# Second pass of a vision tower: side chains over more steps, next group's norm beside the forward scan

## Chip, cores and metric
The kernel runs on one core of one Trainium2 chip. The metric is the device time of one execution in microseconds, the median of several; less is better.

## What is computed
32 images of 96 x 96 are cut into 36 patches each, and with two leading tokens make sequences of 38 tokens of 192 features. Four layers follow, each added to its input after a layer norm: a gated state space layer, a mixture of 8 feed-forward experts (top 2), a bidirectional Mamba layer, and a mixture of 8 linear experts (top 2). The change touches the last two; the reference of the Mamba layer, cut:

```python
def _mamba(x, in_W, conv_w, conv_b, xproj_W, dt_W, dt_b, A_log, Dp, out_W):
    xz = x @ in_W
    xs, z = jnp.split(xz, 2, axis=-1)
...
    u = jnp.transpose(xc, (0, 2, 1))
    x_dbl = u @ xproj_W
    dt, Bm, Cm = jnp.split(x_dbl, [R, R + NS], axis=-1)
    dt = jax.nn.softplus(dt @ dt_W + dt_b)
    A = -jnp.exp(A_log)
    def step(h, inp):
        dt_t, B_t, C_t, u_t = inp
        dA = jnp.exp(dt_t[:, :, None] * A)
        h = dA * h + (dt_t * u_t)[:, :, None] * B_t[:, None, :]
        y = (h * C_t[:, None, :]).sum(-1)
        return (h, y)
...
    y = y * jax.nn.silu(z)
    return y @ out_W
h = x @ down_W + down_b
fwd = _ln(_mamba(h, f_in_W, f_conv_w, ...), f_ln_g, f_ln_b)
bwd = _ln(_mamba(h[:, ::-1], b_in_W, b_conv_w, ...), b_ln_g, b_ln_b)
y = fwd + bwd[:, ::-1]
return y @ up_W + up_b
...
h = h + _L0_attn_ref(_layernorm(h, axis=-1), ...)
h = h + _L0_ffn_ref(_layernorm(h, axis=-1), ...)
h = h + _L1_attn_ref(_layernorm(h, axis=-1), ...)
h = h + _L1_ffn_ref(_layernorm(h, axis=-1), ...)
```

The last mixture takes softmax and top 2 of 8 router scores, and sums the two chosen 192 x 192 products by their weights.

## The kernel before
The 32 images are 4 groups of 8, so a group has T = 304 tokens, features on partitions (128 "main" and 64 "rest"). A first pass does patches, the first scan and the routing of the expert layer; then 27 blocks of tokens go through the experts; the second pass, from about 584 us on, does the Mamba layer and the last mixture. Each engine has its own in-order program, and semaphores tie them.

A group's scan in one direction has 12 steps (QSTEPS). In step n SP reads two tiles of the rows (the step sizes into dA, the inputs into BB, L549; 4 slots, a slot is read again when the scan four steps before is done), ScalarE makes the decay (L813, two steps ahead), VectorE multiplies BB by B (b_product, L1145, one step ahead) and scans (L1159), GpSimd multiplies the states by C (product_step, L679) and TensorE adds them up over states (sum_step). The scan of step n needs the product of n - 2, that product the sum of n - 4 and its own scan.

Around the steps stand side chains, hung on them by hand, one behind another in each engine's program. part_a is the forward scan of group g, part_b the backward one. HOOKS maps step n to the place c of a chain: steps 0, 1, 2, 3, 5, 6, 7, 8. The chains are: the inputs of the next direction (TensorE: project_z, project_taps, project_states, project_steps; ScalarE: inputs, projected, raw_steps, softplus; VectorE: size_of_steps, steps), after which SP writes the rows of that direction to memory (write_rows) and waits for them; the output of the direction just finished (gated_output, direction_out, output_centre, direction_var, output_rstd, output_norm); for the group before, projection up, residual, norm, router, top-2 gates (gates_top, gates_weights, gates_rows), the gates' way through memory (write_gates, read_gates) and the mixture (gate_inputs L699 on GpSimd, mixture on TensorE, add_mixture on VectorE, L1398); for the next group, gathering of the expert rows, combine (L1388), turning back, residual (L1461), norm, projection down. In every engine a chain's place stands behind the scan, product or decay of its step; in TensorE mostly ahead of the sum. The mixture of group g - 1 runs in part_b of g, steps 4 to 9. Roots are computed as exp(-0.5 ln x): Ln and Exp each load a function table (ACT_TABLE_LOAD).

## Time and profile before
| | us |
|---|---|
| median of 3 runs | 1226.91 (1215.95 to 1231.17) |
| the profiled execution | 1218.23, its span 1216.5 |
| TensorE busy | 826.4 (68%) |
| VectorE busy | 711.5 (58%) |
| GpSimd busy | 471.1 (39%) |
| ScalarE busy | 447.5 (37%) |
| TensorE's mean granted clock | 0.767 of 2.4 GHz |

Engines in the rows: PE is TensorE's matmuls, PEld its weight loads, DVE VectorE, ACT ScalarE, POOL GpSimd, SP the engine that issues most transfers. One fp32 matmul appears as two records. An idle time in square brackets stands before the instruction and names what ended it. Times are from the start of the span.

### The profile page before, as it was taken

Reading aid. Unit: us, or ns where it says so; the run is one execution under the profiler, and the core shown is the slowest. Engines: PE = TensorE matmul, PEld = TensorE weight load, DVE = VectorE, ACT = ScalarE, POOL = GpSimd, SP = SyncE. Lnnn points to the kernel's source line nnn. Section 1 sums busy time; section 2 is a strip of 40 time slices with the busy share of each in tenths; the row PEclk is TensorE's granted clock in tenths of the full one; section 3 lists DMA queues with packets and bytes.
Section 4 is the critical chain, followed back from the end, with each engine's and each line's share of the span. In section 5 each row is a group of like instructions: output and inputs, shape, how many; then the busy total and the mean of one; then the engine's idle time right before and its main releaser. Section 6 shows DMA issues by size and latency. Waiting matters only on the chain.

```text
span 1216.5 us, 11333 instructions
## 1 busy us (share of the span) xinstructions
PE 826.4 (68%) x3666; PEld 584.5 (48%) x3666; DVE 711.5 (58%) x978; ACT 447.5 (37%) x847; POOL 471.1 (39%) x300
## 2 busy tenths in 40 slices
PE   3877768767544399999263686657876687657745
PEld 2543435434223388888142455444554465435423
DVE  3199898997982211111116956786748856587720
ACT  2345354444312122222135264545445451443130
POOL 0049446477562200000204634543626344235702
PEclk9778887777655699999676577867977787766957
DMA  9400100000000477676107735557345654347202
GB/s 366 199 30 0 38 1 11 14 1 24 1 4 21 147 227 227 227 227 191 31 16 189 191 103 149 131 145 186 84 124 141 181 127 119 90 131 208 54 0 70
DMA packets 55748, 134.59 MB, mean 111 GB/s; under 512 B 9439, under 2 KB 22150, under 8 KB 54934
## 3 DMA queue, kind: packets, MB, share of 16 engines
q1 hardware_dynamic: 51062, 127.45, 35.9%
q0 software_dynamic: 4496, 6.55, 2.1%
q8 instruction: 23, 0.38, 0.1%
q14 instruction: 23, 0.19, 0.1%
q10 hardware_dynamic: 144, 0.02, 0.0%
HBM read 115.82 MB, written 18.14 MB: 110 GB/s over the span
## 4 chain that ended last, share of the span: by engine, by line
PE 36%; DVE 28%; ACT 10%; issue 9%; DMA 8%; POOL 6%; SPq 2%; DVEq 0%; POOLq 0%; ACTq 0%
PE PS L1491 36%; DVE ST L1128 6%; DMA WXB<-ex_b 4%; DVE ST L1159 3%; DVE BB L1125 3%; POOL PR L679 2%; DVE BB L1121 2%; ACT L735 2%; DMA BB<-rows_d 2%; POOL slots_d L642 1%; DVE BB L1145 1%; POOL xp L665 1%; ACT dA L813 1%; DMA CR<-c 1%; DVE PR L1137 1%
## 5 line engine op out<-in xcount | busy, mean ns | idle before, releaser
L1491 PE MATMUL PS<-PR,CM 128*128 128x152 f32 (+1 forms) x512 | 156.8, 459 | 64.8 <-POOL PR L679 64.5
L1159 DVE TENSOR_TENSOR_SCAN ST<-dA,BB 128x608 f32<-128x608 f32 x96 | 172.2, 1800 | 25.1 <-issue 13.7
L1491 PEld LDWEIGHTS PS<-PR,CM 128*128 128x128 f32 x512 | 111.6, 254 | 100.9 <-POOL PR L679 76.8
L679 POOL TENSOR_TENSOR PR<-ST,q_V 128x608 f32<-128x608 f32 x48 | 86.7, 1814 | 186.1 <-DVE ST L1159 152.9
L813 ACT ACTIVATE dA<-dA,negA 128x304 f32<-128x304 f32 x192 | 93.1, 538 | 146.1 <-DMA BB<-rows_d 145.9
L1491 PE MATMUL PS<-p_S,SEL 128*64 128x152 bf16 (+1 forms) x576 | 83.7, 320 | 70.9 <-DVE PR L1137 37.7
L679 POOL TENSOR_TENSOR PR<-ST,p_V 128x608 f32<-128x608 f32 x48 | 85.3, 1780 | 118.5 <-DVE ST L1159 102.1
L620 POOL TENSOR_TENSOR aP<-dA,p_DL 128x912 f32<-128x912 f32 x32 | 74.4, 2325 | 136.0 <-DVE q_UP L1186 72.3
L912 ACT ACTIVATE HID<-PS,WX 128x128 f32<-128x128 f32 x162 | 47.6, 365 | 137.6 <-PE PS L1491 137.6
L1491 PEld LDWEIGHTS PS<-p_S,SEL 128*64 128x64 bf16 (+1 forms) x576 | 30.3, 120 | 130.6 <-issue 49.5
L1128 DVE TENSOR_TENSOR_SCAN ST<-aP,BB 128x912 f32<-128x912 f32 x32 | 89.2, 2789 | 1.1
L655 POOL DMA_DIRECT2D outs_d<-xp x27 | 14.6, 543 | 162.2 <-DVE xp L1343 162.2
L1491 PE MATMUL PS<-XT,WX 128*128 128x128 f32 x324 | 66.1, 286 | 14.8 <-DMA WXB<-ex_b 11.7
L1491 PE MATMUL PS<-WX,CM 128*128 128x304 f32 x192 | 60.2, 466 | 19.4 <-POOL WX L699 19.3
L1335 DVE COPY XT<-PS 128x128 f32<-128x128 f32 x27 | 7.9, 292 | 104.9 <-PE PS L1491 104.9
L1491 PE MATMUL PS<-HB,CM 96*128 96x152 f32 (+1 forms) x240 | 59.4, 418 | 7.6 <-DVE Or L1399 5.2
L1491 PE MATMUL PS<-XT,WXR 128*128 128x128 f32 x324 | 63.4, 278 | 0.0
L830 ACT ACTIVATE dA<-PS,neg_dt 128x608 f32<-128x608 f32 x64 | 37.4, 635 | 65.5 <-PE PS L1491 65.3
L1491 PEld LDWEIGHTS PS<-XT,WX 128*128 128x128 f32 x324 | 50.0, 195 | 22.1 <-issue 21.3
L1145 DVE TENSOR_TENSOR BB<-BB,q_R 128x608 f32<-128x608 f32 x48 | 45.6, 950 | 22.9 <-DMA BB<-rows_d 22.6
L1491 PEld LDWEIGHTS PS<-HB,CM 96*128 96x128 f32 x240 | 47.6, 240 | 21.3 <-issue 7.8
L1491 PEld LDWEIGHTS PS<-WX,CM 128*128 128x128 f32 x192 | 39.2, 210 | 37.7 <-POOL WX L699 24.4
(340 smaller groups left out, 1728.3 us busy)
## 6 DMA issues: line engine op xcount, KB each, us to landing
dA<-rows_d SPq DMA_DIRECT2D x96, 304.0 KB, 3.7
BB<-rows_d SPq DMA_DIRECT2D x96, 304.0 KB, 4.4
WX<-ex_m SPq DMA_DIRECT2D x27, 963.0 KB
slots_d<-WXR SPq DMA_DIRECT2D x8, 960.0 KB, 27.6
WXR<-ex_r SPq DMA_DIRECT2D x27, 192.0 KB
WX<-gates_d SPq DMA_DIRECT2D x4, 1216.0 KB, 7.4
CM<-c SPq DMA_DIRECT2D x1, 4430.0 KB, 19.8
xp<-x_p SPq DMA_DIRECT2D x4, 864.0 KB, 4.7
```

Of the source, the lines that this page charges most:

```text
L620: nc.gpsimd.tensor_tensor(aP[:, c % 2], dA[:, c % 2], P.DL[:, :].unsqueeze(1).broadcast_to([128, NC, PK]), ALU.mult).then_inc(ap_ready.sem, 1)
L679: nc.gpsimd.tensor_tensor(PRq[:, c % 2], STq[:, c % 2], DIRS[k].Cw.unsqueeze(1).broadcast_to([128, QB, T]), ALU.mult).then_inc(q_product.s ...
L735: nc.scalar.activation(s.RS[0:rows, :], s.VE[0:rows, :], ACT.Exp, scale=-0.5).then_inc(rstd.sem, 1)
L813: last = nc.scalar.activation(dAq[:, slot, i, :], dAq[:, slot, i, :], ACT.Exp, scale=negA[:, j:j + 1])
L830: last = nc.scalar.activation(dA[:, c % 2, :, cols], PS[:, A_BANK:A_BANK + NC, cols], ACT.Exp, scale=neg_dt0[:, h:h + 1])
L912: last = nc.scalar.activation(HX[:, p, f, :], PS[:, WIDE_BANK + 2 * p + h, j * 128:(j + 1) * 128], ACT.Gelu, bias=WX[:, p, FFN + FT * D + ...
L1121: nc.vector.tensor_tensor(BB[:, c % 2], P.WV[:, :].unsqueeze(1).broadcast_to([128, NC, PK]), PS[:, B_BANK:B_BANK + NC, 0:PK], ALU.mult).th ...
L1125: nc.vector.tensor_tensor(BB[:, c % 2], BB[:, c % 2], dA[:, c % 2], ALU.mult).then_inc(b_times_a.sem, 1)
L1128: nc.vector.tensor_tensor_scan(flat(ST, False), flat(aP[:, c % 2], False), flat(BB[:, c % 2], False), 0.0, ALU.mult, ALU.add).then_inc(P.s ...
L1145: nc.vector.tensor_tensor(BBq[:, slot], BBq[:, slot], DIRS[k].Bw.unsqueeze(1).broadcast_to([128, QB, T]), ALU.mult).then_inc(b_times_w.sem, 1)
L1159: nc.vector.tensor_tensor_scan(flat(STq[:, c % 2], back), flat(dAq[:, slot], back), flat(BBq[:, slot], back), 0.0, ALU.mult, ALU.add).then ...
L1491: return nc.tensor.matmul(out, lhsT, rhs, start=first, stop=last)
```

## The change
second_pass now runs part_a once more ahead and once more behind, and part_a gets two more groups: nxt, whose combine, residual and mean now stand in the forward scan at steps 8 to 11 (before: steps 0 to 2 of the backward scan), and mix, whose mixture is finished there. HOOKS is gone; each link of a chain has its own step, one link per step. The norms' roots of the group before and of the next are done together at step 1 of part_b (both_powers), and the logarithm of the step sizes together with the root of the output norm (step_logs), Ln beside Ln and Exp beside Exp. ScalarE writes the size of the steps (Abs) where VectorE did. Top-2 gates move from part_a to steps 4 to 6 of part_b. The six parts of the mixture move from steps 4 to 9 of part_b to its steps 10 and 11 and steps 0 to 3 of the following part_a. The sums of the two directions get a bank each, and the chains banks 5, 7, 4 and 1. TensorE takes the last sum of a direction between z and taps of the next. SP writes the rows of the next direction one step earlier, ahead of its last read, and reads the gates behind them.

```diff
-MIX_PARTS, MIX_FROM = 6, 4
-HOOKS = {0: 0, 1: 1, 2: 2, 3: 3, 5: 4, 6: 5, 7: 6, 8: 7}
+MIX_PARTS, MIX_FROM = 6, QSTEPS - 2
...
-        Y_BANK = 3
+        Y_BANK = (3, 0)
...
-        X_BANK, Z_BANK, AFTER_BANK = 6, (5, 7), (7, 5)
+        X_BANK, Z_BANK, AFTER_BANK, L_BANK, Q_BANK, QR_BANK = 6, 5, 1, 5, 7, 4
...
         def second_pass(eng, part_a, part_b):
 
-
-
-
+            def near(g):
+                return g if 0 <= g < GROUPS else None
+
+            part_a(None, None, 0, None)
             part_b(None, None, 0)
-            part_a(0, None)
-            part_b(0, None, 1)
-            for g in range(1, GROUPS - 1):
-                part_a(g, g - 1)
-                part_b(g, g - 1, g + 1)
-            part_a(GROUPS - 1, GROUPS - 2)
-            part_b(GROUPS - 1, GROUPS - 2, None)
-            part_a(None, GROUPS - 1)
+            for g in range(GROUPS):
+                part_a(g, near(g - 1), near(g + 1), near(g - 2))
+                part_b(g, near(g - 1), near(g + 1))
+            part_a(None, GROUPS - 1, None, GROUPS - 2)
             part_b(None, GROUPS - 1, None)
+            part_a(None, None, None, GROUPS - 1)
...
             load_next(0)
+            write_rows(0, 0)
             for g in range(GROUPS):
-                write_rows(g, 0)
+                rows_there(g, 0)
                 for c in range(QSTEPS):
+                    if c == QSTEPS - 1:
+                        write_rows(g, 1)
                     read_rows(g, 0, c)
-                    if c == 7 and g >= 2:
+                    if c == 10 and g >= 2:
                         store(g - 2)
-                if g >= 2:
-                    store_end(g - 2)
-                write_rows(g, 1)
+                rows_there(g, 1)
                 for c in range(QSTEPS):
+                    if c == QSTEPS - 1 and g:
+                        write_gates(g - 1)
                     read_rows(g, 1, c)
-                    if g and c == SLOTS:
-                        write_gates(g - 1)
-                    if g and c == SLOTS + 1:
-                        read_gates(g - 1)
-                if g + 2 < GROUPS:
-                    load_next(g + 1)
+                    if c == 4:
+                        if g >= 2:
+                            store_end(g - 2)
+                        if g + 2 < GROUPS:
...
+            def part_a(g, tail, nxt, mix):
+                for n in range(QSTEPS):
+                    if g is not None:
+                        product_step(g, 0, n)
+                    if nxt and n == 4:
+                        pool.wait_ge(rows_ready.sem, rows_ready.after(nxt, 1))
+                        pool.sem_inc(turn_taken, 1)
+                    if nxt and n in (4, 5, 6):
+                        gather(nxt, (n - 4,))
+                    if mix is not None and n + QSTEPS - MIX_FROM < MIX_PARTS:
+                        gate_inputs(mix, n + QSTEPS - MIX_FROM)
+
             def part_b(g, tail, nxt):
-                for c in range(QSTEPS):
+                for n in range(QSTEPS):
                     if g is not None:
-                        product_step(g, 1, c)
-                    if tail is not None and 0 <= c - MIX_FROM < MIX_PARTS:
-                        gate_inputs(tail, c - MIX_FROM)
+                        product_step(g, 1, n)
+                    if tail is not None and n >= MIX_FROM:
+                        gate_inputs(tail, n - MIX_FROM)
 
...
+            def both_powers(t, x):
+
+                for s, g, bank in ((Q, t, Q_BANK), (L, x, L_BANK)):
+                    if g is not None:
+                        act.wait_ge(s.ln_var.sem, s.ln_var.after(g, 1))
+                        log_of(s, 128, bank, s.ln_log)
+                for s, g in ((L, x), (Q, t)):
+                    if g is not None:
+                        power_of(s, 128, s.ln_log, s.ln_rstd, g, 1)
 
...
+                    last = nc.scalar.activation(DIRS[k].TM[:, cols], PS[:, Z_BANK, cols], ACT.Abs, bias=cm(d + "dtb", h, h + 1))
...
-            def softplus(g, k):
-
-                s = DIRS[k]
-                act.wait_ge(abs_dt.sem, abs_dt.after(g, k + 1))
-                nc.scalar.activation(s.OM[:, :], s.TM[:, :], ACT.Exp, scale=-1.0).then_inc(exp_dt.sem, 1)
-                act.wait_ge(exp_dt.sem, exp_dt.after(g, k + 1))
-                nc.scalar.activation(LZ, s.OM[:, :], ACT.Ln, bias=1.0).then_inc(log_dt_ready.sem, 1)
+            def step_logs(g, k, out):
+
+                if g is not None:
+                    s = DIRS[k]
+                    act.wait_ge(dt_raw.sem, dt_raw.after(g, k + 1))
+                    nc.scalar.activation(s.OM[:, :], s.TM[:, :], ACT.Exp, scale=-1.0).then_inc(exp_dt.sem, 1)
+                if out is not None:
+                    act.wait_ge(bn_var.sem, bn_var.after(*out))
+                    log_of(Q, BN, AFTER_BANK, bn_log)
+                if g is not None:
+                    act.wait_ge(exp_dt.sem, exp_dt.after(g, k + 1))
+                    if k or not is_first(g):
+                        act.wait_ge(Q.w_ready.sem, Q.w_ready.after(g, k))
+                    nc.scalar.activation(LZ, s.OM[:, :], ACT.Ln, bias=1.0).then_inc(log_dt_ready.sem, 1)
+                if out is not None:
+                    power_of(Q, BN, bn_log, bn_rstd, *out)
...
-            def part_a(g, tail):
+            def part_a(g, tail, nxt, mix):
                 for n in range(QSTEPS):
-                    c = HOOKS.get(n)
                     if g is not None:
                         direction_step(g, 0, n)
-                    if tail is not None and n == 0:
-                        if tail:
-                            add_mixture(tail - 1)
-                        gated_output(tail, 1)
+                    if mix is not None and n == 5:
+                        add_mixture(mix)
+                    if g is not None and n == 6:
+                        if tail is not None:
+                            dve.wait_ge(out_mm.sem, out_mm.after(tail, 2))
+                        steps(g, 1)
                     if tail is not None:
-                        if c == 1:
+                        if n == 1:
+                            gated_output(tail, 1)
+                        if n == 3:
                             output_centre(tail, 1)
-                        if c == 2:
+                        if n == 6:
...
-                        if c == 4:
-                            centre(Q, Q, tail, 0, 5)
-                        if c == 7:
-                            links[Q] = 0
-                            gates_top(Q, tail, 4)
-                    if g is not None:
-                        if c == 3:
-                            size_of_steps(g, 1)
-                        if c == 5:
-                            if tail is not None:
-                                dve.wait_ge(out_mm.sem, out_mm.after(tail, 2))
-                            steps(g, 1)
-                        if c == 2 and not is_last(g):
-                            find_rows(g + 1)
-                    if tail is not None:
-                        if c == 3:
+                        if n == 7:
...
+                        if n == 9:
+                            centre(Q, Q, tail, 0, Q_BANK)
                     if nxt is not None:
-                        if c == 0:
+                        if n == 2 and nxt:
+                            find_rows(nxt)
+                        if n == 8:
                             combine(nxt)
-                        if c == 1:
+                        if n == 10:
                             dve.wait_ge(M.back_T.sem, M.back_T.after(nxt, 1))
                             dve.wait_ge(h_loaded.sem, h_loaded.after(nxt, 32))
                             if g is not None:
...
-                        if c == 2:
-                            centre(L, L, nxt, 0, 5)
-                        if c == 3:
-                            scale(L, nxt, 0)
-                        if c == 5:
-                            size_of_steps(nxt, 0)
-                        if c == 7:
+                        if n == 11:
+                            centre(L, L, nxt, 0, L_BANK)
+
+            def part_b(g, tail, nxt):
+                for n in range(QSTEPS):
+                    if g is not None:
+                        direction_step(g, 1, n)
+                        if n == 1:
+                            gated_output(g, 0)
+                        if n == 3:
+                            if tail is not None:
+                                dve.wait_ge(Q.ln_x.sem, Q.ln_x.after(tail, 1))
+                            output_centre(g, 0)
+                    if nxt is not None and n == 2:
+                        scale(L, nxt, 0)
+                    if tail is not None:
+                        if n == 2:
+                            scale(Q, tail, 0)
+                        if n == 4:
+                            links[Q] = 0
+                            gates_top(Q, tail, QR_BANK)
+                        if n == 5:
+                            gates_weights(Q, tail)
+                            assert links[Q] == Q.chain.per_group, ("Q", links[Q])
+                        if n == 6:
+                            gates_rows(Q, tail, Q_BANK)
+                    if n == 7:
+                        if nxt is not None:
                             if g is not None:
                                 dve.wait_ge(out_mm.sem, out_mm.after(g, 1))
                             steps(nxt, 0)
-                    if g is not None:
-                        if c == 1:
...
+            def part_a(g, tail, nxt, mix):
+                    if n == 0:
+                        if g is not None:
+                            pe.wait_ge(dt_raw.sem, dt_raw.after(g, 1))
+                            project_z(1).then_inc(in_mm.sem, 1)
+                        if tail is not None:
+                            sum_step(tail, 1, QSTEPS - 1)
+                        if g is not None:
+                            pe.wait_ge(bc_copied.sem, bc_copied.after(g, 2))
+                            project_taps(1).then_inc(in_mm.sem, 1)
+                        if n == 2:
+                        if n == 3:
+                            direction_mean(tail, 1)
+                        if n == 5:
+                            direction_var(tail, 1)
+                        if n == 7:
+                            pe.wait_ge(final.sem, final.after(tail, 0))
+                            pe.wait_ge(y_sum.sem, y_sum.after(tail, 1))
+                            mm(PS[:, Q_BANK, 0:T], cm("up", 0, DM, p=BN), YS[:, 0, :], True, True)
+                            mm(PS[:, QR_BANK, 0:T], cm("up", DM, DM + 128, p=BN), YS[:, 0, :], True, True).then_inc(up_proj.sem, 1)
+                        if n == 8:
+                            pe.wait_ge(Q.residual.sem, Q.residual.after(tail, 1))
+                            mean(Q, Q, tail, 0, Q_BANK)
+                        if n == 11:
+                            variance(Q, tail, 0, Q_BANK)
+                    if g is not None:
+                        if n == 3:
+                            project_states(g, 1)
+                        if n == 4:
+                            project_steps(g, 1)
+                    if nxt is not None:
+                        if n == 9:
+                            if g is not None:
+                                pe.wait_ge(dt_raw.sem, dt_raw.after(g, 2))
+                            pe.wait_ge(mixed.sem, mixed.after(nxt, TILES))
+                            back(M, nxt, L_BANK, QR_BANK)
+                        if n == 11:
+                            pe.wait_ge(M.residual.sem, M.residual.after(nxt, 1))
+                            mean(L, L, nxt, 0, L_BANK)
+                    if mix is not None and n + QSTEPS - MIX_FROM - 1 < MIX_PARTS:
+                        mixture(mix, n + QSTEPS - MIX_FROM - 1)
```

SP at the boundary from group 1 to group 2, before. L549 is a read of rows for a step, L534 to L536 are writes of rows, L505 to L509 the load of the next group; the gates of group 0 were read 7 pairs of rows earlier.

```order
L549 DMA BB<-rows_d 128x1x608
L505 DMA KEEP<-keep_d 102x60
L508 DMA m_Hm<-h_md 128x304
L509 DMA m_Hr<-h_rd 64x304
L534 DMA rows_d<-q_DL 128x304
L535 DMA rows_d<-q_DL 64x152
L536 DMA rows_d<-q_DL 64x152
L534 DMA rows_d<-q_WV 128x304
L535 DMA rows_d<-q_WV 64x152
L536 DMA rows_d<-q_WV 64x152
L549 DMA dA<-rows_d 128x1x608
```

The same place now (L548 is the read of rows, L531 to L533 the writes, L553 writes the gates, L558 and L562 read them).

```order
L553 DMA gates_d<-q_LW 8x304
L548 DMA dA<-rows_d 128x1x608
L548 DMA BB<-rows_d 128x1x608
L531 DMA rows_d<-q_DL 128x304
L532 DMA rows_d<-q_DL 64x152
L533 DMA rows_d<-q_DL 64x152
L531 DMA rows_d<-q_WV 128x304
L532 DMA rows_d<-q_WV 64x152
L533 DMA rows_d<-q_WV 64x152
L558 DMA WX<-gates_d 128x2432
L562 DMA WX<-gates_d 64x4x304 x2
L548 DMA dA<-rows_d 128x1x608
```

The gates of group 0 have moved from the middle of the backward reads to the front of the next group's first rows.

TensorE at the head of group 2's forward scan, before. PR are sums of the scan, HB z and taps, p_WV and HID the output product, p_UP and p_Xm the projections, WX the mixture.

```order
L1491 MATMUL PS<-WX,CM 128x304 x4
L1491 MATMUL PS<-PR,CM 128x152 x4
L1491 MATMUL PS<-HB,CM 128x304
L1491 MATMUL PS<-HB,CM 128x152 x2
L1491 MATMUL PS<-HB,CM 128x304 x4
L1491 MATMUL PS<-HB,CM 128x152 x8
L1491 MATMUL PS<-PR,CM 128x152 x4
L1491 MATMUL PS<-p_WV,CM 96x304
L1491 MATMUL PS<-HID,CM 96x304
L1491 MATMUL PS<-p_V,ones_bn 96x304
L1491 MATMUL PS<-p_UP,CM 128x304
```

And now.

```order
L1501 MATMUL PS<-HB,CM 128x304
L1501 MATMUL PS<-HB,CM 128x152 x2
L1501 MATMUL PS<-PR,CM 128x152 x4
L1501 MATMUL PS<-HB,CM 128x304 x4
L1501 MATMUL PS<-HB,CM 128x152 x8
L1501 MATMUL PS<-WX,CM 128x304 x4
L1501 MATMUL PS<-PR,CM 128x304 x2
L1501 MATMUL PS<-WX,CM 128x304 x4
L1501 MATMUL PS<-p_WV,CM 96x304
L1501 MATMUL PS<-HID,CM 96x304
L1501 MATMUL PS<-PR,CM 128x304 x2
L1501 MATMUL PS<-WX,CM 128x304 x4
```

The last sum of the backward scan stands between z and taps, the output product has a sum and two mixture parts ahead of it, and a mixture part stands behind each of the first sums.

TensorE in the backward scan of group 1, now: what stands ahead of the logits turned round (CM,q_LW), for which VectorE's gates_top waits.

```order
L1501 MATMUL PS<-q_Xm,CM 128x304
L1501 MATMUL PS<-q_Xr,CR 128x304
L1501 MATMUL PS<-PR,CM 128x304 x2
L1501 MATMUL PS<-HB,CM 128x304
L1501 MATMUL PS<-HB,CM 128x152 x2
L1501 MATMUL PS<-HB,CM 128x304 x4
L1501 MATMUL PS<-HB,CM 128x152 x8
L1501 MATMUL PS<-CM,q_LW 102x8 x3
```

Before, it stood in the forward scan, with a sum between.

```order
L1491 MATMUL PS<-q_Xm,CM 128x304
L1491 MATMUL PS<-q_Xr,CR 128x304
L1491 MATMUL PS<-PR,CM 128x304 x2
L1491 MATMUL PS<-CM,q_LW 102x8 x3
L1491 MATMUL PS<-PR,CM 128x304 x2
```

Z and taps have come between the router's product and the turned logits.

## Rows read from the trace of the kernel before

**Rows 1.** Stretches: us, busy time of each engine, granted clock, DMA share, GB/s.

```profile
646.20:690.30 44.10, 24.15 (x66) 15.87 (x66) 37.92 (x36) 19.76 (x37) 27.31 (x17) 0.65 0.68 172
690.30:750.60 60.30, 42.38 (x138) 29.11 (x138) 40.73 (x51) 31.13 (x55) 22.64 (x13) 0.70 0.48 123
750.60:815.90 65.30, 41.21 (x142) 29.33 (x142) 46.51 (x75) 32.10 (x58) 30.84 (x19) 0.79 0.57 147
815.90:881.60 65.70, 50.72 (x188) 36.18 (x189) 47.57 (x52) 30.14 (x53) 31.99 (x19) 0.84 0.55 143
881.60:952.30 70.70, 47.41 (x149) 33.14 (x147) 48.14 (x77) 32.09 (x58) 30.84 (x19) 0.74 0.52 133
952.30:1018.00 65.70, 50.82 (x188) 36.31 (x189) 48.38 (x52) 30.13 (x53) 33.20 (x19) 0.84 0.52 139
1018.00:1093.40 75.40, 49.36 (x149) 34.60 (x147) 44.97 (x71) 32.10 (x58) 21.21 (x13) 0.70 0.45 119
1093.40:1146.10 52.70, 37.59 (x124) 26.32 (x125) 45.13 (x33) 15.63 (x30) 38.10 (x19) 0.77 0.59 154
1146.10:1216.50 70.40, 37.64 (x106) 22.32 (x104) 12.30 (x42) 10.05 (x16) 11.22 (x8) 0.64 0.12 34
```

**Rows 2.** VectorE's waits, 646.2 to 1146.1 us: total, times, longest.

```profile
DVE p_TM L1228 <- PE PS L1491: 21.1, 3, 10.0
DVE q_Cm L1245 <- ACT q_RS L735: 20.4, 7, 5.8
DVE BB L1145 <- DMA BB<-rows_d: 16.5, 12, 3.2
DVE q_TM L1205 <- ACT q_DL L797: 14.3, 3, 5.5
DVE ST L1159 <- issue: 13.7, 2, 7.0
```

**Rows 3.** Timeline of TensorE and ScalarE, group 1: start, duration, instruction.

```profile
754.07 6.19 PE L1491 MATMUL PS<-HB,CM 96*128 96x304 f32 x30
...
839.95 0.75 PE L1491 MATMUL PS<-m_Xm,CM 128*96 128x304 f32 x2 [2.24 <-DVE m_Xr L1025]
...
861.13 2.21 PE L1491 MATMUL PS<-WX,CM 128*128 128x304 f32 x8
...
863.75 0.58 ACT L806 ACTIVATE aP<-q_OM 128x456 f32<-128x456 f32 x1
```

**Rows 4.** Timeline of VectorE, scans of groups 0 and 3.

```profile
679.71 2.69 DVE L1159 TENSOR_TENSOR_SCAN ST<-dA,BB 128x608 f32<-128x608 f32 x1
683.00 2.68 DVE L1159 TENSOR_TENSOR_SCAN ST<-dA,BB 128x608 f32<-128x608 f32 x1
...
1127.26 2.69 DVE L1159 TENSOR_TENSOR_SCAN ST<-dA,BB 128x608 f32<-128x608 f32 x1
...
1131.78 2.68 DVE L1159 TENSOR_TENSOR_SCAN ST<-dA,BB 128x608 f32<-128x608 f32 x1
```

**Rows 5.** Timeline, group 1 backward: a free product and a free scan.

```profile
831.82 1.47 POOL L679 TENSOR_TENSOR PR<-ST,p_V 128x608 f32<-128x608 f32 x1 [2.77 <-DVE ST L1159]
...
830.32 1.42 DVE L1159 TENSOR_TENSOR_SCAN ST<-dA,BB 128x608 f32<-128x608 f32 x1
```

**Rows 6.** Side work, group 1: gates (as Rows 1), then groups: busy us, mean ns, idle.

```profile
803.70:809.20 5.50, 2.65 (x13) 1.75 (x12) 4.57 (x23) 1.20 (x4) 1.44 (x2) 1.00 0.51 170
...
L735 ACT ACT_TABLE_LOAD x4 | 5.1, 1283 | 0.1
...
L1214 DVE TENSOR_TENSOR p_OM<-p_OM,p_TM 128x456 f32<-128x456 f32 x1 | 0.6, 634 | 0.0
```

**Rows 7.** Transfers: issues with median us to landing; timeline at the group boundary.

```profile
WX<-gates_d SPq DMA_DIRECT2D x2, 304.0 KB, 10.0
...
873.76 0.32 SPq L534 DMA_DIRECT2D rows_d<-q_DL  x1
...
883.26 1.66 DVE L1145 TENSOR_TENSOR BB<-BB,q_R 128x608 f32<-128x608 f32 x1 [1.68 <-DMA BB<-rows_d]
```

289 lines of the change are left out of this document (114 added, 175 removed).

## Prediction
> **What bounds the kernel now.** I read first the table of stretches, cut at the end of every twelfth scan of the second pass [rows 1]. The eight half-passes take 44.1, 60.3, 65.3, 65.7, 70.7, 65.7, 75.4 and 52.7 us, 499.9 us together; what is ahead of them (646.2 us) is not touched by the change, and 70.4 us follow. VectorE is the busiest engine of every half, but in the six middle ones it stands still for 17 to 30 us (span less busy time). TensorE's granted clock is 0.65 to 0.84 of full, so it spends part of each half at 1.2 GHz and the rest at 2.4 GHz.
>
> Then the waits of VectorE over the eight halves [rows 2]. They aren't for data of the scan, apart from 16.5 us for rows from memory. They are for side work: the gated output waits for TensorE (21.1 us in 3), the root of the output norm for ScalarE (20.4 us in 7), the raw step sizes for ScalarE (14.3 us in 3), and a scan that waits behind the same queue (13.7 us in 2, named "issue"). The longest of each are 10.0, 5.8, 5.5 and 7.0 us. In the backward scan of group 1 it is the pair of 7.0 and 5.5 us: TensorE works through down, z, taps, projections and mixture, 24.4 us from the first of them to the end of the logarithm that they feed (839.95 to 864.33) [rows 3]. At the head of a forward scan it is the sums that stand behind z and taps.
>
> Then what a scan step costs if no side work is late. Two steps without any are 3.29 us apart (679.71 to 683.00) [rows 4]: product 0.7, scan 1.4, and 1.27 us in which the scan is held (2.69 instead of 1.42). In that time GpSimd's own product runs, which takes 1.47 us alone [rows 5]. With a gate input as well on GpSimd the steps are 4.52 us apart (1127.26 to 1131.78) [rows 4], 1.24 more. Where a side operation lies between, GpSimd's product can be over before the scan, and the scan takes 1.42 [rows 5].
>
> That two-input VectorE operations and GpSimd's exclude each other is also what the Trainium skill says (SBUF — State Buffer, Who interferes with whom), and that a VectorE operation with one SBUF input does not; the trace agrees with the first by the 2.69 us, and with the second by the operations that read PSUM at their usual time. The rule speaks against the change: the closer the steps, the more scans are held.
>
> **The change part by part.**
> The bare cost of a half is 12 x 3.28 = 39.4 us. To it comes VectorE's side work [rows 6]: the gates 4.6 busy and some 0.8 between them, 5.4 us, steps 3.4 (four operations of the size of p_OM's 0.63 and some short ones), the gated output 2.0 (three such), combine 1.8, and a scale, centring, norm or residual 0.8 to 1.0 each, two or three operations of under 0.5. Of it some 5 us a half read PSUM and can lie beside GpSimd's product; I take 3 us off for that, between nothing (if they fall at other times) and 5.
>
> The size of the steps leaves VectorE (one operation of 0.63 us, twice a group) and becomes two short ones on ScalarE, hidden in its idle time (it is busy 30 to 32 us of 65 [rows 1]). The roots of the two layer norms share one pair of table loads, the step logarithm and the output's root another. A table load costs 1.28 us, and in group 1 four stand before the Exp of L735 alone [rows 6]; by the order of the instructions 16 loads a group become 10. So 7.7 us of ScalarE's time go, on the path only where VectorE waits for a root, which the new places avoid anyway: none in the sum.
>
> The Trainium skill (ScalarE: Activation LUTs, Table sets) says that one set holds exp and ln, so that ln and then exp would need one load. The trace does not show that: each Exp behind an Ln has its own load. By the page the pairing would save less; the sum takes nothing from it either way.
>
> Now the work that stays, half by half, before and after. "Small" is 1.5 us a half for waits under a microsecond, as those of the residual now (0.7 to 1.3 us).
> - Group 0 forward, 44.1: gets combine, residual and centring of group 1. 39.4 + find 0.9 + steps 3.4 + 3.5 - 3 + small 1.5 + first rows 1.8 = 47.5.
> - Group 0 backward, 60.3: 39.4 + 2.0 + scale 0.8 + 0.4 + 3.4 + 0.8 - 3 + small 1.5, and a wait of 4 us at step 7: down to logarithm took 24.4 us with 3.2 of mixture in it [rows 3], so 21 or 22, and steps 3 to 7 give 18. 49.5.
> - Group 1 forward, 65.3: side work 13.2. No mixture. 39.4 + 13.2 - 3 + 1.5, plus 4 for the gathers on GpSimd, which put 3 us each on steps 4 to 6. 55.5.
> - Groups 1 and 2 backward, 65.7 each: side work 14.0, two gate inputs 2.5, small 1.5. New wait at step 4: VectorE's top-2 choice wants the logits turned round, which TensorE now does behind z and taps (30 records in 6.19 us at best [rows 3]). I take 5 us, between 3.5 (full clock) and 11 (half). And 1 us for the gates at step 10. 60.5.
> - Group 2 forward, 70.7: side work 14.1, four gate inputs 5.0, small 1.5. SP puts the read of the gates (1216 and twice 304 KB, up to 10.0 us to landing [rows 7]) ahead of the first rows of the next group. Counted from step 7: the steps take 4 us, then 9.5 us from their last write to the first product over new rows (873.76 to 883.26 [rows 7]), and 8 more for the gates: 21.5. The four last scans with two gate inputs end at 4 + 13.1 + 2.5 = 19.6. Wait 2. TensorE has z, taps, five mixture parts, projections and five sums in the first five steps: 6.2 + 5 x 2.1 + 4 + 1.4 + 5 x 1.05, 27 us at full clock (a mixture part is 8 records in 2.21 us, a sum half of that [rows 3]), against 22 to 26 on VectorE: a wait of 5, between 0 and 15, and 0.5 in the sum for rounding. 64.5.
> - Group 3 forward, 75.4: the same with side work 9.7: 60.
> - Group 3 backward, 52.7: side work 9.4, two gate inputs instead of six, small 1.5, gates 1. 39.4 + 9.4 - 3 + 2.5 + 2.5 = 51, and 0.5 for the mixture's first part: 51.5.
>
> Sum 47.5 + 49.5 + 55.5 + 60.5 + 64.5 + 60.5 + 60 + 51.5 = 449.5, so 50 us off. The tail grows: mixture parts of group 2 (2.2 us each at full clock, some 4 at 1.2 GHz) now stand in TensorE's queue before the last group's output product, mean and variance, and four gate inputs run behind the last product: 8 us, between 4 and 16. The final mixture and its gates' way through memory stay. 1218.2 - 50 + 8 = **1176 us**. The profiled execution of 1218.2 lies 0.7% under the median of 1226.9, and above the lowest, 1216.0.
>
> **The rivals.**
> - *Stalls only move.* Five stages per group are handed over in order on four in-order queues, and one late link (the logits behind the taps, the sums behind the mixture) holds all. For: the 5 and 15 us ends above. If they come at their upper ends (11 instead of 5 in two backward halves, 15 instead of 5 in two forward ones, tail 14) it is 1176 + 12 + 20 + 6 = 1214: no difference. Against: the waits of up to 10.0 us for the gated output vanish whatever comes, since the gated output is asked for a step later and the sums come ahead of the taps.
> - *The gates' read starves the rings.* If rows only start when the gates have landed (10.0 us), both group boundaries cost 8 us more: 1192. Still faster.
> - *The packing is better than thought.* If the side work covers GpSimd's product in most steps (5 us a half in place of 3) and the small waits are none: 1176 - 28 = 1148.
> - *Slower: TensorE falls to 1.2 GHz in the busiest halves.* Its work in a forward half with mixture is about 39 us at full clock and 78 at half, above the 64 planned; a backward one has 62. Then each of groups 2 and 3 forward takes 78 (+31), the three waits at step 4 and the tail double (+18), and the chain at step 7 is late in groups 0 to 2 (+20): 1245. It decides from where the granted clock of these halves is under 0.6; now they have 0.70 to 0.84, and closer packing gives TensorE less idle time, which speaks against it.
>
> **How the numbers follow.** The forecast (1155 to 1200) gets 0.55, better packing 0.12, the starved rings 0.08, moved stalls 0.17, slower 0.08. The range that leaves out 2 in 10 is 1145 to 1212. A measurement of this kernel, whose three runs span 1.2%, can tell about 2% from no change. Against 1226.9, faster is under 1202: 0.55 + 0.12, and most of the ring case, 0.72; same 0.20; slower 0.08.
>
> **What would show it.** In the profile after: VectorE's waits for L1228, for the output's root and for raw steps shrink to under 3 us each; a new wait at the first gate operation behind a PSUM copy (logits turned), of some 5 us in groups 1 and 2; the last two halves about 60 and 51 us; more scans at 2.69 us than now; 16 loads fewer on ScalarE; the tail at 78 us. Wrong would be: a clock under 0.65 in a middle half, VectorE idle for over 8 us before the add of the mixture at step 5, first rows more than 5 us behind the last scan, or a forward half of group 1 above 60 us.

## The result, and the profile after

The changed kernel takes 1144.23 us (median of 4 runs, 1140.57 to 1146.81), against 1225.1 us (median of 4 by now, 1215.95 to 1231.17) before: a ratio of 0.934 (95% interval 0.928 to 0.941). That is faster, as forecast, but by 81 us where 51 were forecast (1226.9 to 1176), and 0.8 us under the range's lower end (1145). The sum itself started from the profiled execution of 1218.2 us: it took 42 us off, and the profiled execution after (1143.86 us) is 74 us shorter.

The table of stretches of the kernel after, cut again at the end of every twelfth scan (columns as in [rows 1]):

```profile
651.35:696.50 45.15, 26.72 (x73) 17.75 (x74) 41.76 (x43) 23.16 (x45) 26.97 (x17) 0.61 0.76 189
696.50:744.10 47.60, 32.08 (x131) 23.72 (x130) 40.29 (x43) 27.73 (x51) 25.62 (x12) 0.82 0.63 160
744.10:796.20 52.10, 36.21 (x152) 26.72 (x151) 48.77 (x59) 26.30 (x52) 32.69 (x19) 0.85 0.67 171
796.20:847.90 51.70, 34.11 (x135) 24.45 (x134) 45.21 (x67) 28.81 (x55) 24.73 (x12) 0.81 0.62 162
847.90:909.40 61.50, 47.30 (x203) 34.60 (x203) 51.25 (x61) 27.19 (x54) 41.97 (x25) 0.91 0.67 169
909.40:961.00 51.60, 35.62 (x136) 25.56 (x134) 45.29 (x68) 28.81 (x55) 24.75 (x12) 0.80 0.59 158
961.00:1017.50 56.50, 44.66 (x186) 32.50 (x185) 47.38 (x46) 26.19 (x52) 32.28 (x19) 0.94 0.67 169
1017.50:1064.10 46.60, 27.52 (x85) 18.58 (x85) 44.37 (x58) 19.75 (x36) 27.54 (x13) 0.71 0.68 174
1064.10:1142.00 77.90, 46.86 (x153) 31.07 (x153) 15.41 (x42) 10.05 (x16) 20.16 (x14) 0.74 0.11 30
```

The eight halves are 412.7 us together, 87.2 less than the 499.9 of [rows 1]. VectorE's busy time in them (third number after the length) is 364.3 us, before 359.4: its work has not fallen. What it stood still has, from 140.5 us to 48.4. The tail is 7.5 us longer. The first scan starts 5.2 us later, at 651.35 in place of 646.2; 4.7 us of that lie in code that the change doesn't touch. VectorE's last copy of the expert blocks, 0.36 us long, starts at 580.55 before and here at

```profile
585.22 0.36 DVE L1360 COPY xp<-PS 128x192 f32<-128x192 f32 x1 [2.70 <-PE PS L1501]
```

4.7 us later. In the 18 profiled executions below and above (one for each kernel), this copy starts anywhere from 580 to 589 us and the first scan starts from 646 to 656 us, so the start is left out where kernels are compared: "halves" is the time from the first scan to the end of the last. The first half, which begins with the first rows, still varies from 44.8 to 47.0 us between kernels that are alike in it; the last one is 46.6 in eleven of them. A difference in the halves of under 2 us is therefore read without the first half.

VectorE's waits in the halves of the kernel after (total, times, longest), to be read against [rows 2]:

```profile
DVE BB L1166 <- DMA BB<-rows_d: 15.4, 8, 5.6
DVE ST L1180 <- POOL PR L684: 9.4, 7, 1.5
DVE q_gate L1074 <- PE PS L1501: 7.9, 2, 4.1
DVE Om L1415 <- PE PS L1501: 2.4, 2, 1.3
...
DVE p_TM L1229 <- ACT p_OM L819: 1.4, 1, 1.4
DVE q_OM L1231 <- ACT aP L827: 1.4, 1, 1.4
```

Gone are the gated output's wait for TensorE (21.1 us), that for the output's root (20.4), for the raw steps (14.3) and the scans that stood behind the same queue (13.7). Rows from memory are as late as before (15.4 for 16.5), in fewer and longer waits. New is the forecast wait for the turned logits.

### The profile page after: what moved, and what is told of

Read it like the earlier page. It is cut to its first block, busy times and chain, and to the rows that moved or that the text cites. A ratio compares the mean times of both kernels' runs of the same rounds, so it can differ in the third digit from the quotient of the medians.

```text
span 1142.0 us, 11341 instructions
## 1 busy us (share of the span) xinstructions
PE 773.1 (68%) x3666; PEld 556.8 (49%) x3666; DVE 715.8 (63%) x970; ACT 433.3 (38%) x847; POOL 479.6 (42%) x300
## 4 chain that ended last, share of the span: by engine, by line
DVE 31%; PE 30%; issue 12%; DMA 10%; POOL 9%; ACT 6%; SPq 2%; DVEq 0%; POOLq 0%; ACTq 0%
PE PS L1501 29%; DVE ST L1149 6%; DMA WXB<-ex_b 5%; DVE ST L1180 5%; POOL PR L684 4%; DVE BB L1146 3%; DMA BB<-rows_d 3%; DVE BB L1142 2%; DVE BB L1166 2%; POOL slots_d L647 2%; DMA CR<-c 1%; DMA xp<-outs_d,slot_u 1%; POOL q_TM L618 1%; DVE PR L1158 1%; POOL xp L670 1%
## 5 line engine op out<-in xcount | busy, mean ns | idle before, releaser
L1501 PE MATMUL PS<-PR,CM 128*128 128x152 f32 (+1 forms) x512 | 149.6, 440 | 99.2 <-POOL PR L684 99.0
L1180 DVE TENSOR_TENSOR_SCAN ST<-dA,BB 128x608 f32<-128x608 f32 x96 | 166.5, 1739 | 10.9 <-POOL PR L684 9.4
L1501 PEld LDWEIGHTS PS<-PR,CM 128*128 128x128 f32 x512 | 103.0, 237 | 135.4 <-POOL PR L684 115.4
L684 POOL TENSOR_TENSOR PR<-ST,p_V 128x608 f32<-128x608 f32 x48 | 106.5, 2228 | 94.6 <-DVE ST L1180 91.9
L684 POOL TENSOR_TENSOR PR<-ST,q_V 128x608 f32<-128x608 f32 x48 | 84.3, 1759 | 130.4 <-DVE ST L1180 125.7
L1501 PEld LDWEIGHTS PS<-p_S,SEL 128*64 128x64 bf16 (+1 forms) x576 | 29.9, 119 | 134.8 <-issue 48.4
L1166 DVE TENSOR_TENSOR BB<-BB,q_R 128x608 f32<-128x608 f32 x48 | 51.6, 1076 | 25.8 <-DMA BB<-rows_d 25.5
L1501 PE MATMUL PS<-WX,CM 128*128 128x304 f32 x192 | 54.5, 434 | 9.4 <-POOL WX L692 9.4
L1501 PE MATMUL PS<-WX,HID 128*128 128x192 f32 x324 | 57.1, 326 | 0.0
L1501 PEld LDWEIGHTS PS<-WX,HID 128*128 128x128 f32 x324 | 53.5, 190 | 0.0
L1501 PEld LDWEIGHTS PS<-XT,WXR 128*128 128x128 f32 x324 | 51.9, 202 | 0.0
```

The lines of the kernel that those rows point to most:

```text
L684: nc.gpsimd.tensor_tensor(PRq[:, c % 2], STq[:, c % 2], DIRS[k].Cw.unsqueeze(1).broadcast_to([128, QB, T]), ALU.mult).then_inc(q_product.s ...
L1166: nc.vector.tensor_tensor(BBq[:, slot], BBq[:, slot], DIRS[k].Bw.unsqueeze(1).broadcast_to([128, QB, T]), ALU.mult).then_inc(b_times_w.sem, 1)
L1180: nc.vector.tensor_tensor_scan(flat(STq[:, c % 2], back), flat(dAq[:, slot], back), flat(BBq[:, slot], back), 0.0, ALU.mult, ALU.add).then ...
L1501: return nc.tensor.matmul(out, lhsT, rhs, start=first, stop=last)
```

## The experiments

All medians are of four or ten runs; the kernel before, run beside them, had medians of 1218 to 1223 us. "Halves" and waits come from one profiled execution of each kernel, and "more" or "less" is against the kernel after (412.7 us), for labels that begin with b_ against the kernel before (499.9 us). First what the holding by GpSimd costs, since the prediction charged it to every scan.

**short_product**

```diff
-                nc.gpsimd.tensor_tensor(PRq[:, c % 2], STq[:, c % 2], DIRS[k].Cw.unsqueeze(1).broadcast_to([128, QB, T]),
+                nc.gpsimd.tensor_tensor(PRq[:, c % 2, :, 0:16], STq[:, c % 2, :, 0:16], DIRS[k].Cw[:, 0:16].unsqueeze(1).broadcast_to([128, QB, 16]),
```

> The changed kernel (1144.2 us), with GpSimd's product of states and C over 16 of the 304 columns of each block; the rest of the product is left out, so GpSimd no longer holds VectorE in the second pass (but for the gate inputs). It prices all holding at once. The prediction's sum had 12 x 3.28 - 3 = 36.4 us a half for products and scans where VectorE alone needs 12 x 2.1 = 25.2: 11.2 us x 8 = 90 us. If that is what holding costs, the time falls by about 90 us, to 1054. The theory now is that side operations cover GpSimd's product, so that less is held: VectorE's busy time in the eight halves is 364 us now, products and scans free of holding (202) and the side work by the prediction's list (90) make 292, so at most 72 us can go, and as some comes back as waits for rows (2.74 us a step when they are read back to back) I expect -50 to -65, 1079 to 1094.

1100.05 us (1098.35 to 1102.38), halves 370.3. The stretches of group 1 backward and group 2 forward (51.7 and 61.5 us in the kernel after):

```profile
785.40:829.40 44.00, 31.57 (x137) 23.45 (x136) 36.83 (x67) 29.47 (x57) 11.50 (x12) 0.86 0.70 183
829.40:885.90 56.50, 46.08 (x202) 34.69 (x202) 41.87 (x60) 26.45 (x53) 20.01 (x25) 0.96 0.74 192
```

VectorE's busy time falls by 80.5 us over the eight halves (364.3 to 283.8), more than the 72 that I took for the most, yet the halves fall by 42.4 only: waits grow from 48.4 to 86.6 us. Of the 80.5 us that GpSimd takes from VectorE, 38 come back as waits. Waits for rows are the largest of the new ones:

```profile
DVE BB L1166 <- DMA BB<-rows_d: 29.8, 20, 8.1
```

So neither the prediction's price (90 us of time) nor my second guess (50 to 65) was right; it is 44, and that is the most that holding can cost here, since the cut product also hands its result to TensorE earlier.

How much of VectorE's work is held, and where, follows from its busy time for the scans and for the products BB by B alone (this tile's instructions, over the halves; length, then busy time). Before, after, and short_product:

```profile
646.10:1146.10 500.00, 260.12 (x191) 0.76 0.54 139
651.30:1064.10 412.80, 248.80 (x191) 0.81 0.66 169
652.90:1023.30 370.40, 205.34 (x191) 0.85 0.73 187
```

So of the 80.5 us, 43.5 lie on scans and products (248.8 less 205.3), and 37.0 on all the side work (115.5 less 78.5, the rest of 364.3 and 283.8).

**close_output**: the output's chain is put together again, several hand-overs a step.

```diff
-                        if n == 3:
+                        if n == 2:
                             output_centre(tail, 1)
-                        if n == 6:
+                        if n == 3:
                             output_norm(tail, 1)
...
-                        if n == 5:
-                            direction_var(tail, 1)
+                        if n == 3:
+                            direction_var(tail, 1)
```

(the same in part_b, the mean on TensorE and the squares on ScalarE at step 2, and the root on ScalarE at step 3 by itself, with its own Ln and Exp)

> The changed kernel with the spreading of one chain undone: the output of a direction has its product and mean on TensorE at step 2, squares on ScalarE and centring on VectorE at step 2, variance, root and norm at step 3, several hand-overs within a step as before; its root has its own Ln and Exp. Before, VectorE waited 20.4 us in 7 for this root and 7.0 in 4 for the centring. If spreading is what removed these waits, they come back at 2 to 4 us in each of seven halves: the halves' sum (412.7) goes to 427 to 440, the time to 1158 to 1170. The rival: VectorE has other work queued and the waits only change places with others: within 5 us of 1144.

1169.11 us (1166.93 to 1172.19), halves 440.1, 27.4 more. VectorE's waits grow by 35 us while its busy time falls by 8 (364.3 to 356.6); one line holds most of them:

```profile
DVE q_Cm L1264 <- ACT q_RS L742: 30.1, 7, 6.7
```

and the timelines of VectorE and ScalarE in group 1's backward scan show why a step is too short for it:

```profile
818.96 1.42 DVE L1182 TENSOR_TENSOR_SCAN ST<-dA,BB 128x608 f32<-128x608 f32 x1
823.33 0.47 DVE L1264 TENSOR_TENSOR q_Cm<-q_Cm,q_RS 96x304 f32<-96x304 f32 x1 [2.96 <-ACT q_RS L742]
...
818.37 0.46 ACT L863 ACTIVATE q_RS<-q_Cm 96x304 f32<-96x304 f32 x1 [3.35 <-DVE q_Cm L1258]
818.74 0.97 ACT L836 ACTIVATE dA<-dA,negA 128x304 f32<-128x304 f32 x2
819.73 1.28 ACT L738 ACT_TABLE_LOAD   x1
821.02 0.51 ACT L738 ACTIVATE q_VE<-PS,eps_col 96x304 f32<-96x304 f32 x1
821.55 1.28 ACT L742 ACT_TABLE_LOAD   x1
822.84 0.46 ACT L742 ACTIVATE q_RS<-q_VE 96x304 f32<-96x304 f32 x1
```

Squares, decay, load, Ln, load and Exp take 4.9 us on ScalarE (818.37 to 823.30); VectorE has a product and a scan to do meanwhile, 2.1 us. Given three steps or four, as in the change, none of it is seen.

**norm_backward**: combine, residual and mean of the next group back in the backward scan, and its chain two steps later.

```diff
-                        if n == 8:
+                        if n == 8 and g is None:
                             combine(nxt)
...
+                    if nxt is not None and late:
+                        if n == 0:
+                            combine(nxt)
...
-                    if n == 7:
+                    if n == 7 + late:
```

(The two norms' roots are taken apart at three boundaries, and SP's store_end and load_next move from step 4 to 7 with it.)

> The changed kernel with one part undone: combine, residual and mean of the next group at steps 0, 1 and 2 of the backward scan, as before, and what hangs on them two steps later (scale at 4, inputs at 6, size of the steps and the output's norm at 9); each link still has a step of its own. VectorE's work is the same. If it is the early start of this chain that lets the spread chains end in time, the rows of the next group are written two steps (8 to 10 us) later, and the wait for the first rows grows by that at three boundaries: 24 to 30 us, 1168 to 1175, the heads of groups 1 to 3. The rival: where the norm stands doesn't matter once every link has its own step: 1150 or less.

1171.6 us (1168.86 to 1173.27), halves 436.4, 23.7 more. Its waits for rows:

```profile
DVE BB L1172 <- DMA BB<-rows_d: 34.6, 11, 11.3
```

19.2 more than after. The start of the chain in the forward scan, and so the time at which SP can write the next rows, is worth what was expected (24 to 30 us; 27 by the medians).

**b_hooks_spread**: the kernel before, with its chains over more steps and nothing else.

```diff
-HOOKS = {0: 0, 1: 1, 2: 2, 3: 3, 5: 4, 6: 5, 7: 6, 8: 7}
+HOOKS = {0: 0, 1: 1, 3: 2, 4: 3, 6: 4, 8: 5, 9: 6, 10: 7}
```

> The kernel before (1225 us) with one idea of the change alone: the eight places of the chains over more steps (0, 1, 3, 4, 6, 8, 9, 10 instead of 0, 1, 2, 3, 5, 6, 7, 8), nothing else moved. The halves have 17 to 30 us in which VectorE stands still for side work. If the gain of the change is mostly that each link has a step or more between it and the next, this gives a large part of it: 25 to 45 us, 1180 to 1200. The rival: the later chains end later too (rows of the next direction written after the scan's end), so the wait moves to the first rows of each half: 1215 to 1240.

1231.16 us (1228.84 to 1240.72), a ratio of 1.014 (1.005 to 1.023) to the kernel before; halves 506.2, 6.3 more. Two lines of its waits:

```profile
DVE BB L1145 <- DMA BB<-rows_d: 47.9, 14, 8.5
...
DVE q_Cm L1245 <- ACT q_RS L735: 9.6, 4, 3.9
```

The root's wait is halved (20.4 in [rows 2]), but that for rows trebles (16.5): the rival. Spreading these eight places alone doesn't pay; with the earlier start that norm_backward takes away, it does.

**b_sum_first**, **sum_behind_taps** and **sum_late_gated_early** are about the last sum of the backward scan. b_sum_first is the kernel before with this alone:

```diff
                 if g is not None:
                     project_z(1).then_inc(in_mm.sem, 1)
+                if tail is not None:
+                    sum_step(tail, 1, QSTEPS - 1)
+                if g is not None:
                     pe.wait_ge(bc_copied.sem, bc_copied.after(g, 2))
                     project_taps(1).then_inc(in_mm.sem, 1)
-                if tail is not None:
-                    sum_step(tail, 1, QSTEPS - 1)
```

> The kernel before (1225 us) with one part of the change alone: TensorE takes the last sum of the backward scan between z and taps of the next. VectorE's wait for it was 21.1 us in 3. With the sum ahead of the taps (24 of 30 records) the wait loses the taps' 4 to 7 us each at TensorE's clock there: 12 to 21 us, 1204 to 1213, if nothing else is late then. The rival: it is the chain behind the taps (inputs, projections, raw steps, root of the output) that holds the head, and the wait only moves to those: 1220 or more.

1204.2 us (1195.03 to 1211.23), 0.989 (0.985 to 0.993) of before; halves 478.4, 21.5 less, and the wait is 7.4 us in 2. The profiled execution is the fastest of its ten (1195.03 us); by the medians the gain is 15 us.

```profile
DVE p_TM L1228 <- PE PS L1491: 7.4, 2, 4.2
```

sum_behind_taps is the changed kernel with the reverse of this diff.

> The changed kernel with one part undone: TensorE takes the last sum of the backward scan behind z and taps, as before, not between them. Before, VectorE waited 21.1 us in 3 for that sum (10.0 at the longest). The gated output now stands at step 1, one step later. Taps are 24 records, 4.3 us at full clock. If the order is what removed the wait, it comes back at some 3 us in each of groups 1 to 3, 9 to 12 us, 1153 to 1156; the fallback is the later gated output: if that alone covers it, 1144 to 1147.

1145.62 us (1143.68 to 1148.5), halves 412.1: nothing lost, and the later gated output is enough alone. sum_late_gated_early adds

```diff
-                        if n == 1:
+                        if n == 0:
                             gated_output(tail, 1)
```

> The changed kernel with two parts undone: the last sum of the backward scan behind z and taps, and the gated output that reads it at VectorE's step 0, not 1. With the sum behind the taps alone nothing was lost (halves 412.1 in place of 412.7), while in the kernel before the sum ahead of them alone won 21.5 us of its halves. If either of the two is enough to hide the sum, this one shows the wait again: 4 to 6 us in each of groups 1 to 3, halves 425 to 431, 1156 to 1162. The rival: the wait was of TensorE's other load in the kernel before, and is gone whatever the order: within 3 us of 1144.

1150.04 us (1147.5 to 1154.74), halves 419.6, 6.9 more (1.6 of them in the first half, which the edit doesn't reach), and `p_TM` waits again:

```profile
DVE p_TM L1245 <- PE PS L1501: 8.5, 3, 3.6
```

Two parts of the change act on the same wait, and with the later gated output in place the sum's order gives nothing; the reverse, the sum first with the gated output early, was not run in the changed kernel. With both gone it is 5 to 7 us, half of what I expected or less. That TensorE has less ahead of it than in the kernel before would explain this, but it wasn't tested.

**short_mixture** and **b_short_mixture** leave most of the mixture out, of the kernel after and of before:

```diff
                 for i in (2 * part, 2 * part + 1):
+                    if part and part < MIX_PARTS - 1:
+                        continue
...
-                nc.gpsimd.tensor_tensor(GX[:, 2 * part:2 * part + 2, :], GX[:, 2 * part:2 * part + 2, :],
+                nc.gpsimd.tensor_tensor(GX[:, 2 * part:2 * part + 2, 0:16], GX[:, 2 * part:2 * part + 2, 0:16],
```

> The changed kernel with most of the last mixture left out: gate inputs over 16 of 304 columns, and TensorE's products of parts 1 to 4 of 6. The forward halves of groups 2 and 3 (61.5 and 56.5 us) have mixture, that of group 1 (52.1) has none. The prediction took 5 us of gate inputs and 5 of waiting for TensorE for it. If the sum over VectorE's and GpSimd's work is right, group 2 falls to 52 to 53, group 3 to 48 to 49 (4 us less side work), and the tail loses 8 us of gate inputs and 9 of products: together 30 to 38 us, 1106 to 1114. The rival: what lengthens these halves is the gates' read, which stays in: group 2 stays above 57.

1125.46 us (1120.35 to 1130.13), halves 405.6: group 2's forward half 57.7, group 3's 52.6, each 3.8 less where I expected 9 and 8. VectorE's busy time there falls by 5.7 and 8.3 us (51.25 to 45.52, 47.38 to 39.07), so the gate inputs take what the prediction charged (5 us) or more; waits take part of it back. In the three backward halves for which the prediction charged 2.5 us each VectorE's busy time doesn't move (45.21 and 45.26, 45.29 and 45.24, 44.37 and 44.47). That group 2 stays at 57.7 is the rival's number, with 6.3 us of waits for rows at its head as before (6.0), and the rest of it stays open. Of the 18 us that the profiled execution lacks, 11 lie in the tail (66.9 in place of 77.9).

> The kernel before with most of the last mixture left out, as in the run of the changed kernel: gate inputs over 16 of 304 columns, and TensorE's products of parts 1 to 4 of 6. There its halves fell by 6.6 us (412.7 to 406.1). Here the mixture stands beside down, z, taps and projections of the backward scan, 24.4 us from down to the logarithm with 3.2 of mixture in it. If its move to the forward scan is a part of the gain, its price is larger here: the three backward halves of groups 1 to 3 lose 5 to 8 us each, 15 to 24 together. The rival: it is hidden there as well, and the halves fall by less than 7.

1203.09 us (1197.29 to 1210.01), halves 486.0, 13.9 less; the backward halves of groups 1 to 3 lose 6.6, 3.7 and 7.3, 17.6 together, and group 2's forward half gains 4.9. By the halves the mixture cost 14 us where it stood and costs 7 where it stands. The medians don't bear this out: the whole time falls by 15.5 us here and by 18.8 in the changed kernel, and 10.1 and 11.0 of that lie in the tails, which leaves 5 and 8 for the rest. What its move is worth, between nothing and 7 us, is not shown.

**gates_later** reads the gates behind the second pair of the next rows, **gates_early** ahead of the writes:

```diff
-                if g + 1 < GROUPS:
-                    write_rows(g + 1, 0)
                 if g:
                     read_gates(g - 1)
+                if g + 1 < GROUPS:
+                    write_rows(g + 1, 0)
```

> The changed kernel with the gates read behind the second pair of rows of the next forward scan instead of ahead of the first, and the six mixture parts at steps 0 to 5 of that scan (GpSimd) and 1 to 6 (TensorE), the addition at step 7. If the read of the gates (1.8 MB) is what keeps the first rows back (VectorE waits 4.3, 1.3 and 0.4 us for them at the head of group 2), the waits for rows, 15.4 us in 8, fall by 8 to 10 us, and the time to 1134 to 1137. The rival: the read takes the same share of the queues a few steps later, and the waits for rows move to steps 3 to 5, or the addition waits at step 7: 1141 to 1150.

1149.63 us (1147.28 to 1152.71), halves 419.1, 6.4 more: the wait for rows is one of 4.6 us at the head of group 2, in place of 4.3, 1.3 and 0.4, and GpSimd's and TensorE's mixture is later by a step and a half.

> The changed kernel with one move on SP: the gates are read ahead of the writes of the next rows, not behind them. SP waits 3 to 5 us for those rows (from 832.7 to 837.0 in group 1's backward scan), and the read of the gates would lie in that time. If the read beside the first rows is what holds the heads of groups 2 and 3 (VectorE waits there 4.3 + 1.3 + 0.4 us for rows), each loses 3 to 5 us and the halves' sum falls from 412.7 to 403 to 407. The rival, from the last kernel with the gates read later (heads no shorter: one wait of 4.6 in place of 4.3 + 1.3 + 0.4): the way from the last write through memory to the first product over new rows (10 us) is the bound there, and the halves stay within 2 us.

1141.68 us (1139.75 to 1144.64), halves 411.7; group 2's forward half is 61.4, group 3's 54.7. SP's own timeline around it:

```profile
835.60 0.60 SPq L548 DMA_DIRECT2D BB<-rows_d  x1
837.87 0.34 SPq L558 DMA_DIRECT2D WX<-gates_d  x1
838.25 1.30 SPq L562 DMA_DIRECT2D WX<-gates_d  x2
840.53 0.33 SPq L531 DMA_DIRECT2D rows_d<-q_DL  x1
...
843.43 0.62 SPq L533 DMA_DIRECT2D rows_d<-q_WV  x1
848.57 0.56 SPq L548 DMA_DIRECT2D dA<-rows_d  x1
```

The rows are now written beside the gates' read: SP's first read of rows follows 4.5 us after the end of its last write, where it follows 2.1 us after it in the changed kernel, with the issues of the gates between. VectorE waits 2.3 and 1.4 us at that head and not 6.0 in all, but group 2's half is as long; only group 3's is 1.8 shorter. The wait is paid in other places.

**logits_first** moves logits_T on TensorE ahead of z and taps; **both_moves** is this with gates_later, **early_and_logits** with gates_early.

> The changed kernel with one move on TensorE: the logits turned round stand ahead of z and taps at step 4 of the backward scan, not behind. VectorE waits for them 7.9 us in 2 (4.1 the longest). If the order on TensorE is the cause and nothing else is as late, both waits go and the time falls by 6 to 8 us, to 1136 to 1138. The rival: z, taps and the chain behind them (inputs, projections, raw steps, logarithm) are as late, so the wait turns up at step 7 before the size of the steps, and in more held scans: 1141 or more.

1145.02 us (1141.86 to 1148.95), halves 413.3, of which the first half is 1.6 more than after. The wait for the logits is gone, and the two backward halves lose 1.3 and 1.0 us, not 4. Two lines of its waits:

```profile
DVE ST L1180 <- POOL PR L684: 12.3, 9, 1.5
...
DVE q_gs L1096 <- ACT q_gs L778: 3.8, 2, 2.0
```

The next link (the ratio on ScalarE) is late instead, by 1.9 us each.

> The two moves together: logits turned ahead of z and taps, and gates read behind the second pair of rows with the mixture one and a half steps later. If both waits are independent and on the path, the gains add: 14 to 18 us, 1126 to 1130. If each only uncovers the other's slack, no more than the larger of the two, about 1136.

1148.47 us (1143.41 to 1149.04), halves 420.0: no sum of gains.

> The changed kernel with two moves: gates read ahead of the writes of the next rows, and the logits turned round ahead of z and taps. Alone the first gave 1.7 us in the halves and the second none (2.3 us less in two backward halves, 1.6 more elsewhere). If gains add it is 1139 to 1142; the rival, that each frees time that the next link takes, 1142 to 1145.

1140.38 us (1137.48 to 1142.41), halves 412.4. Without the first half, its halves are 1.6 us less than those of the changed kernel (gates_early alone: 2.3 less, logits_first: 1.0 less); the medians differ by 0.3%, which the start's scatter covers.

**unpaired** takes the two norms' roots one behind the other, each with its Ln and Exp, **one_bank** lets both directions sum into one bank:

```diff
-                for s, g, bank in ((Q, t, Q_BANK), (L, x, L_BANK)):
+                for s, g, bank in ((L, x, L_BANK), (Q, t, Q_BANK)):
                     if g is not None:
                         act.wait_ge(s.ln_var.sem, s.ln_var.after(g, 1))
                         log_of(s, 128, bank, s.ln_log)
-                for s, g in ((L, x), (Q, t)):
-                    if g is not None:
                         power_of(s, 128, s.ln_log, s.ln_rstd, g, 1)
...
-        Y_BANK = (3, 0)
+        Y_BANK = (3, 3)
```

> The changed kernel with the roots and logarithms unpaired again on ScalarE: Ln and Exp of the next group's norm, then Ln and Exp of the other; Exp and Ln of the step sizes, then Ln and Exp of the output's root. Two more pairs of table loads in most halves, 1.28 us each. The prediction took nothing for the pairing. If ScalarE's time is covered it is 1142 to 1147 us. The rival: the roots and the logarithm are on the path at steps 2, 6 and 7 (now 5.0 us of waits in 5 for ScalarE at the size of the steps), and each extra load adds 1.3 us to some of them: 10 to 20 us, 1154 to 1164.

1148.27 us (1141.09 to 1150.37), halves 412.5: covered. It has only 4 table loads more (46 in the eight halves, against 42), and not the two pairs in most halves that were expected. Its edit also puts the output root's Ln behind the logarithm of the step sizes, but there Ln still stands beside Ln (Exp, Ln, Ln, Exp), so nothing is unpaired; only the norms' roots at two boundaries are. It says that these 5 us of ScalarE lie off the path, no more.

> The changed kernel with one part undone: both directions sum into one bank, and the first sum of a direction waits until the gated output of the one before has read it (VectorE's step 1). The product of step 2 waits for that sum. If the second bank is what lets sums and gated output pass each other, each half's head gains a wait of 2 to 3 us: 16 to 24 us over eight halves, 1160 to 1168. The rival: the sum of step 0 is wanted only by the product of step 2, by when the gated output is done: within 3 us of 1144.

1145.99 us (1142.81 to 1149.88), halves 414.8. Of the 2.1 us more, 1.9 are in the first half, where kernels alike vary as much; the other seven are as in the kernel after (367.8 for 367.6). The second bank gives nothing that can be seen.

## Why the prediction was right in kind and short in size

**The waits.** Working back through its sums, the prediction left 51 us of waits in the halves (449.5 less 398.3 of work); 48.4 are there. Those at the head of [rows 2] are gone. The turned logits cost 4.1 us at the longest (5 forecast, 3.5 to 11 the bounds), and the logarithm in group 0's backward scan 0.9 + 1.4 (4 forecast). At the heads of groups 2 and 3 the two shares were wrong and their sum nearly right: rows 6.0 and 7.2 us (2 forecast), TensorE's mixture 1.3 and 1.1 (5 forecast). That the sum of all waits came out within 3 us is thus partly luck: 4 us for the rows' start too little, 4 for the mixture too much, twice. And one of the prediction's own signs of being wrong came up, first rows more than 5 us behind the last scan: 5.6 us at the head of group 3 (961.0 to 966.6). TensorE's granted clock was 0.91 and 0.94 in these halves. The gathers cost group 1's forward half nothing (4 forecast).

**The work: the step that failed.** The sum put 398.3 us of VectorE's work into the halves; it is 364.3. That term is the whole error: 1176 - 34.0 (work) - 2.8 (waits) + 5.2 (start) - 0.5 (tail 7.5, not 8) = 1143.9. "The bare cost of a half is 12 x 3.28" took every scan for held by GpSimd, less 3 us a half. That puts 291.2 us (315.2 less 24) on scans and products; they take 248.8. Without holding they take 205.3 (short_product), as priced (201.6), so what was wrong is the holding: 89.6 us charged to them, 43.5 measured. The page of the kernel after shows that most scans aren't held:

```profile
L1180 DVE TENSOR_TENSOR_SCAN ST<-dA,BB 128x608 f32<-128x608 f32 x96 | 166.5, 1739 | 10.9 <-POOL PR L684 9.4
```

1739 ns each, 0.32 us over the free one (1.42 in [rows 5]); the mean was 1800 before, so the forecast "more scans at 2.69 us than now" is wrong too. The side work was priced at 107.1 us, gate inputs included, and takes 115.5, 37.0 of it holding. So the term is off by -42.4 + 8.4 = -34.0: some of the holding that the sum put on scans and products falls on the operations of its list instead. The list itself was too dear for free operations (without the product they take 78.5 us): the gates' 5.4, for one, contained 0.8 us of idle time between them and one 102x24 operation held for 0.8 us,

```profile
804.22 0.96 DVE L1057 TENSOR_TENSOR q_gate<-q_gate,q_gs 102x24 f32<-102x24 f32 x1
```

which takes 0.18 where it is free.

One smaller error is seen. The gate inputs of steps 10 and 11 were charged to the backward halves, but GpSimd does them when the gates have landed:

```profile
849.66 1.47 POOL L692 TENSOR_TENSOR WX<-WX,q_Xm 128x608 f32<-128x608 f32 x1 [0.49 <-DMA WX<-gates_d]
851.09 1.47 POOL L684 TENSOR_TENSOR PR<-ST,p_V 128x608 f32<-128x608 f32 x1
852.52 2.02 POOL L692 TENSOR_TENSOR WX<-WX,q_Xm 128x608 f32<-128x608 f32 x1
```

behind the half's last scan (847.9), while VectorE waits for rows. By short_mixture gate inputs cost VectorE 14.0 us in all, where the sum had 17.5.

The check that would have caught it stands in [rows 1]: VectorE's busy time over the eight halves was 359.4 us, all holding of the time in it, and the change moves nearly all of this work from half to half without adding to it; the sum had 398.3. Busy 359.4 and waits 51 would have given 410 for the halves, against 412.7. That this check comes so near is in part a balance of two changes: scans and products fell by 11.3 us (260.1 to 248.8), side work rose by 16.2 (99.3 to 115.5), since more of the holding now falls on it.

**The tail** grew by 7.5 us (8 forecast). All of it stands ahead of the output norm, which comes 15.1 us behind the last scan before and 22.6 after; what follows takes as long as before. The gated output starts 2.6 us later (6.8 in place of 4.2 us behind the last scan), waiting for TensorE's last sum, and takes 3.1 us longer, beside GpSimd's gate inputs. The wait, and the gated output's last operation after and before:

```profile
DVE p_TM L1245 <- PE PS L1501: 6.8, 1, 6.8
...
1074.35 1.49 DVE L1250 TENSOR_TENSOR HID<-p_TM,aP 64x152 f32<-64x152 f32 x1
...
1151.81 0.31 DVE L1233 TENSOR_TENSOR HID<-p_TM,aP 64x152 f32<-64x152 f32 x1
```

That TensorE's mixture parts cause the rest is argued, and short_mixture speaks against it in part: with four of six parts left out the way from last scan to output norm is 20.9 us, the wait for the last sum 9.5, not 6.8, at a granted clock of 0.64 until its end where it is 1.00 in the kernel after; b_short_mixture has 15.5.

**The rivals.** "Stalls only move" (1214) fell: they went. But it is right about what is left, as logits_first and both_moves show. "Better packing" (1148) was the nearest, for one of its two reasons: side work does take up much of GpSimd's product (43.5 us of holding on scans and products, not 89.6), but the small waits did not vanish. "Starved rings" holds in place (6.0 and 7.2 us at two heads) but neither reading the gates later nor earlier shortens those halves by more than 2 us. TensorE's clock rose in the forward halves with mixture (0.74 to 0.91 and 0.70 to 0.94 by the rows) instead of falling. The rule of the Trainium skill on the lock between GpSimd and VectorE (SBUF — State Buffer, Who interferes with whom) agrees with the trace, with 80.5 us of VectorE's time as its size here. Read as an argument against closer packing it misled: the steps stand closer, and scans and products are held less.

**Where the 87 us came from.** Undone alone, from the kernel after: the spread output chain 27.4 us, the norm beside the forward scan 23.7, the two remedies for the last sum 5 to 7. These are some 57 us of the halves (by the medians 24.9, 27.4 and 5.8, some 58). They don't add strictly (the sum's order alone gave 21.5 us of the halves and 15 of the median in the kernel before, and spreading alone -6.3). Second bank and paired norm roots give nothing that the halves show, and the worth of the mixture's place is not shown. The other 30 us are the interplay of these and of parts not undone: the gates' choice in the backward scan, the size of the steps on ScalarE, residual and norm of the group before. They stay open.

## What to carry to other kernels

Price moved work from busy time that the profile already has for that stretch, holding included, and forecast only the waits anew; a sum built from single steps should reproduce the stretch before the change before it is trusted for the one after. Don't charge an interference to every step when the prices of the other operations were read beside it: it is then counted twice. A chain of hand-overs wants steps between its links, and it must also start earlier by as much, or its end is late: here spreading without the early start lost 6 us, and either one undone cost 24 to 27. When the busiest engine's waits are down to one or two for each cause, removing a single one (4 us) gives 1 us.

## What the runs showed of the hardware

- Holding is mutual and hits small operations too. GpSimd's product takes 1.47 us alone and up to 4.3 beside VectorE (in the row below, VectorE does a product, a scan and a product meanwhile), and a 102x3 operation of VectorE that takes 0.16 us took 1.26 in the backward scan of group 1:

```profile
872.36 4.33 POOL L684 TENSOR_TENSOR PR<-ST,q_V 128x608 f32<-128x608 f32 x1 [2.06 <-DVE ST L1180]
...
824.77 1.26 DVE L1101 SCALAR_TENSOR_TENSOR q_gs<-q_gs 102x3 f32<-102x3 f32 x1
```

- Taking 80.5 us of holding off the busiest engine gave 42.4 us of its stretch. Of the holding, 43.5 us lay on scans and products and 37.0 on side work.
- The same instructions ahead of the second pass end up to 9 us apart between executions (the last copy of the expert blocks starts at 580.2 to 589.3 us), while the last half, where an edit doesn't reach it, repeats to 0.1 us (46.6 us, eleven times). The first half doesn't (44.8 to 47.0). In the changed kernel and its variants, stretches tell small differences that whole times can't; for the kernel before there is one profiled execution only, and each set of its whole times spans 13 to 22 us.
